# x centred by a matmul from a second copy of the input, token rows turned in 32x32 blocks on VectorE, loads over 128 partitions

## The reference

```
y   = layernorm of x over the 64 channels, pixel by pixel            (eps 1e-6)
h   = relu(w1 @ groupnorm(y, 8 groups) + b1)                         per pixel
x1  = x + y + w2 @ h + b2
t   = x1 as 16384 rows (tokens) of 64
z   = layernorm of t over its 64
for each of 32 experts: the 8 tokens of the image with the largest gate logit
      (softmax over all tokens), pooled, through a 64-256-64 network with gelu,
      and the result added to those 8 rows, scaled by the token's probability
out = t + these additions, as an image again
```

## Time and profile before

| | us |
|---|---|
| median of 3 runs (lowest, highest) | 627.55 (625.82, 629.17) |
| span of the profiled execution | 630.2 |

### The profile page before, as it was taken

One profiled execution on the slowest core, in us unless ns is written; L12 is line 12 of the kernel. 1 busy time (PEld: TensorE's weight loads), 2 busy tenths in 40 slices (PEclk: granted clock), 3 DMA queues, 4 the chain that ended last, 5 costly groups with the idle time before them and its releaser, 6 DMA issues.

```text
span 630.2 us, 14170 instructions
## 1 busy us (share of the span) xinstructions
PE 541.1 (86%) x5732; PEld 274.7 (44%) x5732; DVE 487.1 (77%) x950; ACT 436.5 (69%) x651; POOL 188.7 (30%) x116
## 2 busy tenths in 40 slices
PE   3659999998989898998999899989898988977982
PEld 1333444444444444444444444434443433344762
DVE  5575565789888978897899779987888798799520
ACT  2455788787977796779767976897687855974110
POOL 1008362115302440235022602080308044130045
PEclk9956998999999989998999799989998999976595
DMA  8960245623661457144714453435411265520000
GB/s 193 196 152 14 101 129 158 170 80 91 189 179 62 109 156 190 57 136 134 200 70 135 133 157 113 136 101 167 134 43 61 91 182 152 160 81 5 6 16 19
DMA packets 26752, 73.38 MB, mean 116 GB/s; under 512 B 4152, under 2 KB 4152, under 8 KB 22592
## 3 DMA queue, kind: packets, MB, share of 16 engines
q1 hardware_dynamic: 25664, 71.44, 41.2%
q0 software_dynamic: 1024, 1.05, 0.6%
HBM read 38.40 MB, written 34.08 MB: 115 GB/s over the span
## 4 chain that ended last, share of the span: by engine, by line
PE 44%; DVE 28%; ACT 12%; issue 11%; DMA 2%; another core or an unknown queue 1%; POOL 0%; SPq 0%; ACTq 0%; DVEq 0%; POOLq 0%
PE st L372 10%; PE cv L383 8%; PE bc L494 6%; PE tl L400 6%; PE cv L391 5%; DVE us L949 5%; ACT junk L810 5%; DVE xs L959 5%; DVE lg L947 3%; PE tl L409 3%; DVE cnd L1041 2%; DVE top_i L1046 2%; ACT tok L775 2%; DVE us L951 2%; DMA xs<-in_x 2%
## 5 line engine op out<-in xcount | busy, mean ns | idle before, releaser
L1437 POOL TENSOR_TENSOR xs<-xs,us 128x1024 f32<-128x1024 f32 x64 | 150.7, 2376 | 360.3 <-DVE xs L959 177.4
L959 DVE SCALAR_TENSOR_TENSOR xs<-cv,vecs,xs 128x1024 f32<-128x1024 f32 x64 | 82.0, 1282 | 25.2 <-PE cv L391 24.9
L770 ACT ACTIVATE hid<-cv,b1n 128x1024 f32<-128x1024 f32 x64 | 71.3, 1115 | 39.3 <-PE cv L383 38.8
L803 ACT ACTIVATE sqc<-us 128x1024 f32<-128x1024 f32 x64 | 67.6, 1056 | 42.3 <-DVE us L949 41.6
L400 PEld LDWEIGHTS tl<-ident,xs 128*128 128x128 f32 x512 | 64.4, 196 | 56.9 <-issue 56.9
L951 DVE CUSTOM_DVE_ANT_0 us<-us,bc 128x1024 f32<-128x1024 f32 x60 | 73.0, 1216 | 19.0 <-PE bc L494 17.7
L949 DVE TENSOR_TENSOR us<-xs,bc 128x1024 f32<-128x1024 f32 x60 | 73.0, 1216 | 17.5 <-PE bc L494 17.1
L810 ACT ACTIVATE junk<-us 128x1024 bf16<-128x1024 f32 x64 | 67.5, 1055 | 20.5 <-DVE gsum L951 19.9
L372 PE MATMUL st<-xs,stat_w 128*32 128x256 f32 x1024 | 72.6, 404 | 8.9 <-DMA xs<-in_x 8.9
L400 PE MATMUL tl<-ident,xs 128*128 128x128 f32 x512 | 77.1, 296 | 1.6 <-ACT lg L785 1.6
L409 PE MATMUL tl<-xs,gcen 128*32 128x256 f32 x1024 | 71.7, 400 | 7.4 <-ACT tok L775 7.4
(11 more groups left out here) (210 smaller groups left out, 657.0 us busy)
## 6 DMA issues: line engine op xcount, KB each, us to landing
xs<-in_x SPq DMA_DIRECT2D x64, 512.0 KB, 7.0
out_rows<-tok SPq DMA_DIRECT2D x64, 512.0 KB
us<-in_e_w SPq DMA_DIRECT2D x8, 260.0 KB
xs<-in_e_w SPq DMA_DIRECT2D x8, 256.0 KB
sqc<-out_rows,idx_all POOLq DMA_INDIRECT x16
out_rows<-sqc,idx_all POOLq DMA_INDIRECT x16
vecs<-in_b SPq DMA_DIRECT2D x4, 0.2 KB, 14.0
gate_bias<-in_gate_b SPq DMA_DIRECT2D x4, 0.1 KB, 12.4
```

The lines of the kernel that those rows point to most:

```text
L959: nc.vector.scalar_tensor_tensor(out=xu, in0=cv[:], scalar=vecs[:, 3:4], in1=xu, op0=ALU.add, op1=ALU.add).then_inc(x1_done, 1)
L1437: nc.gpsimd.tensor_tensor(xu, xu, su, ALU.add).then_inc(s_done, 1)
```

## The change

Four things change together.

1. *Centring.* The host gives a second copy of x (`raw`), with the two 512-column pieces of a unit exchanged against the halves. SP loads it into `us` itself, unit by unit. TensorE multiplies each unit by `cen` = I - 1/64 into PSUM (`centre_into`, four products of 64x64 by 512, as conv1) and a copy brings the centred x back into `us`: on ScalarE for images 2 to 7 (`centre_copy`, through `tl`, for image n in steps 2 to 7 of iteration n - 2 and steps 0 and 1 of n - 1), on VectorE for images 0 and 1 (the C jobs, through `bc`). The sums of x, the means and their spreads leave.
2. *Tokens.* Instead of eight TensorE transposes and a ScalarE copy, VectorE transposes a unit in 32x32 blocks (`turn`) straight from `xs` into `tok`. The output then holds each token as two rows of 32; the host puts them together. Each gather and each scatter of 128 tokens becomes two indirect DMAs of 128 half rows, with a second list of indices (+1024).
3. *Loads.* x comes in an order in which a quarter of an image is one DMA over 128 partitions (1 MB); `raw` comes in units of 512 KB over 128 partitions. The first two images are loaded without a wait.
4. *Places.* The spreads, the search (`VALUES_AT`, `PLACES_AT`, `EXPLOG_AT`) and the squares move to other steps; the fold and the merge of an image's candidates move from step 7 of an iteration to steps 0 and 1 of the next. In the last iteration the search keeps its places.

The core of the diff:

```diff
-C_JOBS = {(0, 0): 0, (0, 1): 1, (0, 2): 2, (1, 0): 3, (2, 0): 4, (2, 1): 5, (2, 2): 6, (3, 0): 7}
-S_JOBS = {(4, 0): 0, (4, 1): 1, (4, 2): 2, (5, 0): 3, (5, 1): 4, (5, 2): 5, (6, 0): 6, (6, 1): 7}
-L_JOBS = {(1, 1): 0, (1, 2): 1, (3, 1): 2, (3, 2): 3}
+C_JOBS = {(0, 0): 0, (0, 1): 1, (0, 2): 2, (1, 0): 3, (1, 1): 4, (1, 2): 5, (2, 0): 6, (2, 1): 7}
+S_JOBS = {(3, 1): 0, (3, 2): 1, (4, 0): 2, (4, 1): 3, (5, 0): 4, (5, 1): 5, (6, 0): 6, (6, 1): 7}
+L_JOBS = {(1, 1): 0, (1, 2): 1, (2, 1): 2, (3, 0): 3}
-M_JOB, LAST_M_JOB = (7, 0), (7, 1)
+M_JOB = (0, 1)
+LAST_M_JOB, TAIL_M_JOB = (7, 1), (7, 0)
-VALUES_AT = {1: 0, 2: 1, 3: 2, 4: 3}
-PLACES_AT = {2: 0, 3: 1, 4: 2, 5: 3}
+VALUES_AT = {2: 0, 4: 1, 5: 2, 6: 3}
+PLACES_AT = {3: 0, 4: 1, 5: 2, 6: 3}
...
+def centre_of(it, s):
+    n, k = (it + 2, s - 2) if s >= 2 else (it + 1, s + 6)
+    return (n, k) if 2 <= n < NB else None
...
+            def load(b, m):
+                cols = slice(2 * UN * m, 2 * UN * (m + 1))
+                sp.dma_start(xs[b % 2][:, cols], x[b, :, cols]).then_inc(x_in[b % 2][m], 16)
+            def load_raw(b, k):
+                cols = slice(UN * k, UN * (k + 1))
+                sp.dma_start(us[b % 2][:, cols], raw[b, :, cols]).then_inc(raw_in[b % 2][k], 16)
...
             for m in range(NG):
-                sp.wait_ge(sumx_done, m + 1)
-                load(1, m, 1)
+                load(0, m)
+            for k in range(NU):
+                load_raw(1, k)
+            for m in range(NG):
+                load(1, m)
...
+                if it + 2 < NB:
+                    sp.wait_ge(c_done, NU * it + s + 1)
+                    sp.wait_ge(s_done, NU * it + s + 1)
+                    load_raw(it + 2, s)
                 if b >= 0:
                     store(b, u)
...
-                for k in range(8):
-                    mm = pe.transpose(tl[:, P * k:P * k + P], unit(xs[par], u)[:, k:UN:8], ident[:])
-                mm.then_inc(t_done, 1)
+            def centre_into(out, par, k):
+                for sl, h in ((0, 0), (1, 1), (0, 1), (1, 0)):
+                    r = slice(C * sl, C * sl + C)
+                    mm = pe.matmul(out[C * h:C * h + C, CH * sl:CH * sl + CH], cen[r, r], half_chunk(us[par], k, sl, h),
+                                   start=True, stop=True)
+                return mm
+            def centre(it, s):
+                if centre_of(it, s):
+                    n, k = centre_of(it, s)
+                    pe.wait_ge(raw_in[n % 2][k], 16 * (n // 2 + 1))
+                    pe.wait_ge(lcopy_done, NU * it + s - 1)
+                    centre_into(tl, n % 2, k).then_inc(cen_done, 1)
...
-            def token_copy(b, u):
+            def centre_copy(it, s):
+                if centre_of(it, s):
+                    n, k = centre_of(it, s)
+                    act.wait_ge(cen_done, centres_before(it, s) + 1)
+                    nc.scalar.activation(unit(us[n % 2], k), tl[:], ACT.Copy).then_inc(cen_copied, 1)
...
-                    ins = nc.vector.tensor_tensor(unit(us[n % 2], k), unit(xs[n % 2], k), stat[:], ALU.subtract)
+                    ins = nc.vector.tensor_copy(unit(us[n % 2], k), stat[:])
...
+            def turn(b, u):
+                dve.wait_ge(x1_done, NU * b + u + 1)
+                wait(dve, stored[u % 2], 16 * ((NU * b + u) // 2))
+                nc.vector.transpose(tok[u % 2][:], unit(xs[b % 2], u)).then_inc(tok_done, 1)
...
+                if b >= 0 and not (s == NU - 1 and p1):
+                    turn(b, u)
                 x1(it, par, s)
...
+                if s == 0 and it >= 2:
+                    merging[it - 2] = merge_pixels(it, it - 2)
+                if s == 1 and it >= 2:
+                    merge_values(it - 2, merging.pop(it - 2))
...
             for b, g in SCATTERS:
                 pool.wait_ge(row_ready, 1 + [b0 <= b < b1 for b0, b1 in ADDS].index(True))
                 wait(pool, scattered[b], 16 * before[b])
-                nc.gpsimd.indirect_dma_start(
-                    outs[b], bass.IndirectOffsetOnAxis(ap=idx_all[:, b, g:g + 1], axis=0),
-                    rows_all[:, b, g, :], None).then_inc(scattered[b], 16)
-                before[b] += 1
+                for i in range(2):
+                    nc.gpsimd.indirect_dma_start(
+                        outs[b], bass.IndirectOffsetOnAxis(ap=idx_all[i][:, b, g:g + 1], axis=0),
+                        rows_all[:, b, g, 32 * i:32 * i + 32], None).then_inc(scattered[b], 16)
+                before[b] += 2
```

More of the change, by code:

```diff
@@ L116, in mk_metaformer_kernel @@
         hid = sb("hid", [P, UN])
-        tok = [sb(f"tok{i}", [P, HALVES, 8, C]) for i in range(2)]
+        tok = [sb(f"tok{i}", [P, UN]) for i in range(2)]
         sqc = sb("sqc", [P, SQC * UN])
@@ L175, in mk_metaformer_kernel @@
         pxf = sb("pxf", [P, GATHERS])
-        idx_all = sb("idx_all", [P, NB, GATHERS], U32)
+        idx_all = [sb(f"idx_all{i}", [P, NB, GATHERS], U32) for i in range(2)]
         px_all = sb("px_all", [P, NB, GATHERS])
@@ L306, in _ @@
         def _(sp):
[L307 to L313, removed]
+            def load(b, m):
[5 more added lines that the diff above has]
+            for k in range(NU):
+                load_raw(0, k)
             for vec, src in enumerate((gn_w, gn_b, b1, b2)):
@@ L365, in _, with sum_group @@
         def _(pe):
-            def sum_group(dst, src, m, ring, first):
+            def sum_group(dst, src, m, ring, first, tall, wide):
                 for sub in range(2):
@@ L484, in spread_stat @@
                     return
+                if kind == "C":
+                    centre_into(out, n % 2, k).then_inc(bc_filled, 1)
+                    return
                 for i in range(2):
@@ L576, in prologue @@
             def prologue():
-                for m in range(NG):
-                    first_x_sums(m)
-                    for k in (2 * m, 2 * m + 1):
-                        spread_stat(-1, "C", k)
-                    if m >= 1:
-                        xc_square_sums(0, m - 1)
+                for k in range(NU):
+                    spread_stat(-1, "C", k)
+                    if k % 2 == 1 and k >= 3:
+                        xc_square_sums(0, (k - 3) // 2)
                 pe.wait_ge(w_in, 16 * 18)
@@ L882, in step @@
                 square_at(it, (s, 1))
+                if s != 2:
+                    centre_squares(it, s)
+                if s == 2 and p1:
+                    ln1_rsqrt(n)
                 if not p1 and s in (5, 6):
@@ L1166, in step, with search @@
                         diagonals(DIAGS_AT.index(s))
+            def search(t, s, p1):
+                if not p1:
+                    if s in LAST_PLACES_AT:
+                        top_places(t, LAST_PLACES_AT[s])
+                    return
+                if s in VALUES_AT:
+                    top_values(t, VALUES_AT[s])
+                if s in PLACES_AT:
+                    top_places(t, PLACES_AT[s])
             lns = Steps(dve, ln_steps, 0)
@@ L1286, in _ @@
             norm_bias(0)
-            mean(1, 0)
             for it in range(NB):
@@ L1485 @@
     ins = {
-        "x": np.ascontiguousarray(x).reshape(NB, C, PIX),
+        "x": np.asarray(x).reshape(NB, C, HALVES, HW).transpose(0, 2, 1, 3).reshape(NB, P, HW),
+        "raw": np.asarray(x).reshape(NB, C, HALVES, NU, 2, CH).transpose(0, 4, 1, 3, 2, 5).reshape(NB, P, HW),
         "gn_w": L0_conv_gn_w, "gn_b": L0_conv_gn_b,
@@ L1501 @@
     for name in names:
[L1502 removed]
+        args.append(nc.dram_tensor(name, (2 * PIX, C // 2), F32, kind="ExternalOutput").ap())
     mk_metaformer_kernel(nc, *args)
     r = run_bass_kernel_spmd(nc, [arrays], core_ids=[0])
[L1505 to L1506 removed]
+    got = np.stack([r.results[0][name] for name in names]).reshape(NB, NG, 2, HALVES, 2, 32, 2, 2, 8, 32)
+    return np.ascontiguousarray(got.transpose(0, 4, 9, 3, 1, 6, 2, 7, 8, 5)).reshape(NB, C, 128, 128)
```

235 lines of the change are left out of this document (104 added, 131 removed).

## The result

The changed kernel takes 650.28 us (median of 4 runs, 648.15 to 652.37), the kernel before 628.22 beside it: a ratio of 1.035, 95% interval 1.032 to 1.038. Slower, as forecast (647, range 622 to 668). The two traces span 646.3 and 630.2 us, so they show 16.1 us of the 22 by which the medians differ. A span is about 2 us shorter than the time of the same execution: the trace of the changed kernel is its fastest timed run, 648.15. The kernel before was traced in a long execution: the 44 other executions of it on record span 622.5 to 628.9.

A forecast was written before the change was run, and what follows sets the result against it. TensorE was nearest to full, but not alone: steps are rings through one PSUM tile, and GpSimd's scatter issues end last. 630.2 - 7 - 1 + 5.6 + 22.5 = 650, so 647 against the median; range 622 to 668.

The forecast's parts named there:

- The tail: End of the kernel: 32 scatter issues on GpSimd instead of 16, with a later gather and last turn, +22.5 us.
- +2.6 for the last gather: Tail: image 7's gather issues 2.6 us later on GpSimd; about 1.3 of it reaches the first scatter.
- Iterations 1 to 6: The six iterations after the first take 382 us against 389, a gain of 7.
- the walk: One steady iteration followed queue by queue, step by step: 62.9 us against 64.9, or 64.4 with one clock fall.
- the 0.75 of the value merge: Step 1 of a steady iteration: 0.75 us of value merge leaves, helping make the step 9.5 for 9.7.
- Rival E: Steady iterations: TensorE falls to 1.2 GHz twice per iteration on the path, +10 us, 657; chance 0.09.
- Iteration 7: Last iteration: no subtraction to remove, so turns are extra; with merge and copies +5.6 us, bounds +2 and +9.
- The start and iteration 0: Before and in the first iteration: start gains about 3 us, iteration 0 loses 2; together -1.
- A: Rival for steady iterations: engines overlap fully, 59.5 us each, no clock fall; 621 or 619 us, chance 0.12.
- B: Rival for the tail: a half-row DMA costs GpSimd half, tail +2.5, 630 or 627 us; chance 0.08.
- C: Rival for loads: those over 128 partitions stay near 220 GB/s, about 665 us; chance 0.09.
- D: Rival for VectorE: a turn takes 2.5 us, +55, 703 us; chance 0.06.

The follow-up runs named there:

- e2: The kernel before, with its 16 scatters issued as 32 scatters of half rows, gathers left whole: 645.96 us, ratio 1.029 to the kernel before.
- e3: The kernel before, with each quarter of an image loaded by one DMA over 128 partitions instead of two over 64: 625.10 us, ratio 0.9965.
- e9: The kernel before with 128-partition loads and, for image 0 alone, the changed kernel's centring: 621.23 us, ratio 0.986 to the kernel before.
- e1: The changed kernel with the second half rows not written back, 16 scatters instead of 32: 629.96 us, ratio 1.003 to the kernel before.
- e6: The changed kernel with GpSimd's adds of units 6 and 7 moved behind step 3's x1, except for the last image: 650.87 us, ratio 1.035.
- e10: The changed kernel with GpSimd's adds of units 6 and 7 later (not the last image's) and idle TensorE products where it waits: 635.83 us, ratio 1.016.
- e11: The changed kernel with idle TensorE products where it waits, GpSimd's adds kept in place: 642.85 us, ratio 1.022 to the kernel before.
- e4: The changed kernel with GpSimd's adds of units 6 and 7 moved behind step 3's x1 for every image: 661.77 us, ratio 1.055 to the kernel before.
- e5: The changed kernel with turns over 512 columns instead of 1024, half the tokens left out of the output: 626.09 us, ratio 0.998.

## Why the prediction was right, and where it was not

*The tail* (+22.5, measured +21.2) carried the forecast. The price of an issue held: 31 distances of 1.275 and 0.97 are 40.5, in e2 as in the changed kernel. The +2.6 for the last gather is there too, in VectorE's wait for its rows (0.68 in the earlier trace rows):

```profile
583.43 0.42 DVE L1250 TENSOR_REDUCE tr<-sqc 128x4 f32<-128x256 f32 x1 [3.63 <-DMA sqc<-out_rows,idx_all]
```

This is 37.9 us after the last x1, 35.1 in the kernel before. But at the first scatter the difference is gone (53.3 in both). The trace of the kernel before hides it: its granted clock from the last x1 to the first scatter is 0.65, and 0.74 in the changed kernel. With whole gathers the same stretch takes 51.4 to 52.6 us in e2, e3 and e9 (clock 0.70 to 0.74), with half-row gathers 53.3 to 55.1 in e1, e6, e10 and e11 (0.72 to 0.74), some 2 us more, for the 2.45 counted (1.3 for the gather and 1.15 for the turn). So the term as a whole agrees better than its parts in this pair of traces: 2.5 us that the prediction did not have lie behind the last issue.

*Iterations 1 to 6* (-7, measured -4.8, in a pair of traces that leaves 2 to 3 us open): the prices held. Steps 0, 1, 5, 6 and 7 are 6.3, 9.6, 7.3, 7.3 and 8.7 for 6.5, 9.5, 7.3, 7.3 and 8.85; step 3 is 8.2 for 8.55, step 4 7.82 for 7.85 where the clock holds. Step 0 on TensorE, with the centring second in the row, as the earlier trace rows:

```profile
356.92 1.09 PE L424 MATMUL cv<-us,w1n 64*64 64x512 f32 x8 [1.10 <-DVE b1n L1045]
357.80 1.07 PE L440 MATMUL tl<-us,cen 64*64 64x512 f32 x8
358.79 1.07 PE L413 MATMUL st<-xs,stat_w 128*32 128x256 f32 x16
359.68 1.05 PE L413 MATMUL st<-sqc,stat_w 128*32 128x256 f32 x16
360.66 1.09 PE L432 MATMUL cv<-hid,w2bd 64*64 64x512 f32 x8
```

Step 2 is 8.3 to 8.5 (once 9.8) where the walk with its fall of the clock had 8.5, and that agreement is half an accident. The step that failed is "the 0.75 of the value merge": I moved 0.75 us of small instructions from one place to another without asking what runs beside them. They took 3.7 there; without the stretch VectorE is busy 54.2 us in an iteration of e10, near the 55 predicted. The fall I counted was seen too: ten falls in iterations 1 to 6, counted by microsecond, where the kernel before has five. Rival E (two falls per iteration) thus nearly came true in number; it did not add up to its price, because in step 2 the fall and the stretched pair lie side by side. e10, with neither, gives 62.1 for the walk's 62.9. Beside the 64.1 of the kernel before where its clock doesn't fall (iterations 2 and 3 of e2), that is 2.0 us saved in an iteration, the difference that the walk had; the pair and the falls took it back.

The Trainium skill, "SBUF — State Buffer", section "Who interferes with whom", says that VectorE and GpSimd share one pair of ports, that a VectorE instruction with two SBUF inputs contends with a GpSimd instruction that reads SBUF, that a tensor_scalar can contend as well, and that the one that comes second blocks until the first is done. The trace agrees: 1.52 and 1.87 us up to the ends of the adds, while the reduction between them kept its 0.17. It is a page that the prediction should have weighed.

*Iteration 7* (+5.6, though its three terms add to 5.8; measured +7.6): step 1 grew by 4.15 (3.8 counted). Step 2 grew by 3.84 where 1 was counted; it holds the same pair, stretched by 3.0, and is 8.42 instead of 10.42 in e4, where the pair is not stretched. The other six steps together gave 0.4 back, but against the 51.6 us of e2, e3 and e9 they cost 1.1, near the 1 counted, and the whole iteration 9.1, at the upper bound. Hidden is not the word for the turns there: with half turns (e5) five of these six steps, all but step 0, are 0.2 to 0.5 us shorter. The turns used up the time in which VectorE had waited, and VectorE's work now sets these steps.

*The start and iteration 0* (-1, bounds -6 and +5; measured -7.9): the largest miss, outside its bounds. The load rate was right in kind (416 GB/s, I had taken 370). The failed step is "TensorE has cold centring products to do in place of spreads: about 3 gained": I set the products against the spreads by their busy time, and left out that sums, mean and spread of a quarter wait for each other, which is part of what bounded the start. e9 prices the change of chain at 5.2. "Cold" holds for the first two products alone (1.98 and 1.83 us, then 1.09, while the granted clock reads 1.00), and the sums that they replace were slow for longer. So the 5.2 holds a second thing that I left out: the products bring TensorE to full speed sooner.

Rivals: A (overlap, 59.5 us an iteration) is refuted by the 62.1 of e10, where neither a fall nor the stretched pair is left. B by e2, C by the 416 GB/s, D by the 1.24 us of a turn, half of the 2.49 that the prediction estimated from the Trainium skill's 311 ns, a figure for bf16 there. (D's sum, 703, should be 702.) The misses of the terms, -7, +2, +2 and -1, partly cancelled each other; the forecast of the whole is better than its parts, and that is luck.

What stays open: why a fall of the clock comes in some iterations and not in others. The timed runs of the changed kernel differ with it: the fastest, which was traced, has a mean granted clock of 0.883, the three others 0.875 to 0.880.

## What to carry to other kernels

An indirect DMA on GpSimd was paid by the issue here, not by the byte (rows of 256 and of 128 bytes); a layout that splits a row in two doubles the bill where GpSimd ends last. A small instruction has no price of its own: when it is moved, look at what runs beside it in the new place, on GpSimd above all. And an initial load is worth what the chain behind it can use: here some 9 us of faster landing (an estimate: 4.2 MB at 218 and at 431 GB/s) gave 3, and another way of centring gave 5.

## What the runs showed of the hardware

- VectorE instructions on 16 and 2 elements that waited, counted as busy, for the end of a GpSimd add: 1.52 and 1.87 us instead of 0.17 and 0.23.
- TensorE's clock fell during or just after single waits of 1.6 to 1.9 us (all ten falls in iterations 1 to 6 of the changed kernel; 1.94 us before the one at 375, and 1.78 before the one at 194 in e4), though not after each of them; with idle products in those waits it stayed at 2.4 GHz through iterations 2 to 5, in e10 and e11 alike.
- TensorE's first products took twice their later time (1.98 and 1.83 us, then 1.09) in rows whose granted clock reads 1.00.
- A turn of 128x1024 in 32x32 blocks costs VectorE as much as any pass over 1024 float32 columns (1.24), half of it 0.70.
